# A four-layer block with attention and experts: maxima split by VectorE, squares by ScalarE, matrix steps at other hooks, rows of three tiles fetched at the border, first v products in group 0

## What is computed

```
x = x + attention(x)      # 16 heads of 16, masked softmax, projection Wo, RMS norm, gain and shift
x = x + experts(x)        # gate over 8 experts, best 2 of them, three layers 256-512-512-256 each, ReLU
x = x + spectral(x)       # x @ basis * cond -> orthogonalised 64x64 matrix -> * cond -> output basis
x = x + quaternions(x)    # fixed rotation of groups of features, gated
```

## Time and profile before

| | |
|---|---|
| median of three runs | 1247.67 us |
| profiled execution, its own time | 1257.77 us |
| its span | 1255.7 us |
| TensorE busy (PE) | 1152.4 us, 92% |
| VectorE busy (DVE) | 839.8 us, 67% |
| ScalarE busy (ACT) | 718.7 us, 57% |
| GpSimd busy (POOL) | 553.5 us, 44% |
| mean granted clock of TensorE | 0.977 |

### The profile page before, as it was taken

The page is one execution under the profiler, slowest core; times in us unless marked ns, Lnnn a source line. Parts: engine busy times, 40 slices in busy tenths (PEclk is TensorE's granted clock), DMA queues, the critical chain, the costliest instruction groups (busy, mean ns, idle before and its releaser), DMA issues.

```text
span 1255.7 us, 23441 instructions
## 1 busy us (share of the span) xinstructions
PE 1152.4 (92%) x7533; PEld 777.1 (62%) x7590; DVE 839.8 (67%) x2395; ACT 718.7 (57%) x1504; POOL 553.5 (44%) x869
## 2 busy tenths in 40 slices
PE   8899999989999899997877999878999999999978
PEld 4333434334344343432316989878999999999968
DVE  4888688897888978886843434535555567844447
ACT  3466666665656656564554556535555566566645
POOL 7324245674756748567372465441122212122210
PEclk9899999999999999998989999979999999999999
DMA  7835646348464484543535488942554666832636
GB/s 204 240 122 173 201 143 196 134 161 243 161 184 140 152 239 157 169 155 127 210 128 194 112 295 272 278 118 43 178 143 113 190 212 169 277 61 48 172 85 201
DMA packets 101456, 213.52 MB, mean 170 GB/s; under 512 B 10885, under 2 KB 71181, under 8 KB 92886
## 3 DMA queue, kind: packets, MB, share of 16 engines
q1 hardware_dynamic: 87030, 193.34, 47.5%
q0 software_dynamic: 14304, 18.69, 8.2%
HBM read 239.15 MB, written 74.29 MB: 250 GB/s over the span
## 4 chain that ended last, share of the span: by engine, by line
PE 65%; issue 7%; POOL 7%; DVE 7%; DMA 4%; SPq 4%; ACT 3%; another core or an unknown queue 1%; DVEq 0%; POOLq 0%; ACTq 0%
PE bank L1017 33%; PE bank L1117 6%; PE bank L1086 6%; PE bank L1098 5%; PE bank L1102 4%; PE bank L1062 3%; DVE junk L1534 2%; PE bank L1135 2%; SPq L876 2%; DMA w_parts<-in_W 2%; POOL ssq L790 1%; POOL xw L1803 1%; PE bank L1032 1%; ACT full L1336 1%; PE bank L1175 1%
## 5 line engine op out<-in xcount | busy, mean ns | idle before, releaser
L1272 ACT ACTIVATE pt<-bank 128x512 f32<-128x512 f32 x512 | 301.9, 596 | 191.9 <-PE bank L1102 137.9
L1534 DVE CUSTOM_DVE_ANT_0 junk<-bank,mneg 128x512 bf16<-128x512 f32 x512 | 336.4, 684 | 82.5 <-PE bank L1086 81.7
L1885 POOL DMA_INDIRECT x<-yout,rows x78 | 122.9, 1575 | 327.0 <-ACT yout L1341 309.8
L1681 DVE TENSOR_TENSOR hid<-full,hid 128x256 fp32r<-128x256 f32 x312 | 133.8, 432 | 170.1 <-ACT full L1336 158.4
L1017 PE MATMUL bank<-hid,w 128*128 128x256 f32 x1872 | 237.1, 284 | 6.9 <-DVE hid L1681 5.2
L1017 PEld LDWEIGHTS bank<-hid,w 128*128 128x128 f32 x1872 | 226.7, 191 | 7.7 <-issue 5.8
L1331 ACT ACTIVATE hid<-bank,biases 128x256 fp32r<-128x256 f32 x312 | 150.7, 483 | 127.5 <-PE bank L1017 106.3
L1336 ACT ACTIVATE full<-bank,biases 128x256 f32<-128x256 f32 x312 | 150.2, 481 | 0.0
L1102 PE MATMUL bank<-mneg,identb 128*128 128x512 bf16 x391 | 149.9, 383 | 0.0
L1017 PE MATMUL bank<-rowsT,w 128*128 128x256 f32 x936 | 128.9, 290 | 0.3 <-issue 0.3
L1117 PE MATMUL bank<-pt,vaug 128*17 128x512 f32 x1024 | 125.8, 610 | 2.2 <-ACT pt L1272 0.7
(11 more groups left out here) (184 smaller groups left out, 1479.4 us busy)
## 6 DMA issues: line engine op xcount, KB each, us to landing
w<-split_weights SPq DMA_DIRECT2D x80, 1024.0 KB
w<-split_weights SPq DMA_DIRECT2D x40, 2048.0 KB
split_weights<-w_parts SPq DMA_DIRECT2D x64, 512.0 KB, 4.8
w_parts<-in_W SPq DMA_DIRECT2D x64, 256.0 KB, 4.9
split_parts<-parts SPq DMA_DIRECT2D x28, 384.0 KB, 3.5
rows<-routed SPq DMA_DIRECT2D x39, 258.0 KB, 3.4
stacks<-split_parts SPq DMA_DIRECT2D x36, 256.0 KB, 7.5
qst<-split_parts SPq DMA_DIRECT2D x24, 256.0 KB, 7.5
```

Of the source, the lines that this page charges most:

```text
L1272: A.activation(pt[n % len(pt)][:, :], bank[3 + n % 2][:, :], ACT.Exp, scale=float(D) ** -0.5).then_inc(exped.sem, 1)
L1534: V.tensor_tensor_reduce(junk[n % 2][:, :], bank[n % 3][:, :], mneg[:, 0, st, :], 1.0, FLOOR, ALU.add, ALU.max, rowmax[gi % 2][:, hh, st:s ...
L1681: V.tensor_tensor(lo, h[:, :], hi.bitcast(F32), ALU.subtract).then_inc(hidden_low.sem, 1)
L1885: G.indirect_dma_start(x2_dram, bass.IndirectOffsetOnAxis(ap=rows[j % NS][:, tt, E + 1:E + 2].bitcast(U32), axis=0), yout[j % 2][:, tt], N ...
```

## The change

1. `split_maxima` is done by VectorE (one copy, then a subtraction that waits for it), at the same place in the list.
2. `square_o` and `square_x1` are done by ScalarE, as an activation Square with an accumulated output.
3. In `chain`, six empty hooks stand between `count` and `place` instead of four, and for batch 6 nine instead of six between `residual` and `scale`.
4. The v products of batch 0 leave the prologue and alternate in group 0 with the projections of batch 1; in the first two groups two entries of `todo` are worked off after each k.
5. The matrix steps stand after layer 2 steps 0 and 2, layer 1 step 1 and layer 3 step 0. Their generator yields four times before its first piece (`MATRIX_PAUSE`).
6. Fetching rows and fetching biases are steps of their own. At `near` the rows and biases of tile 0 and the rows of tile 1 are fetched; after the end of attention come rows and biases of tile 2, then biases and weights of tile 1, then tiles 3 and 4. The second rows buffer moves into the memory that is free at `near`, and both output buffers out of it.

```diff
--- before.py
+++ after.py
@@ -59,6 +59,7 @@
 CHUNKS = NX * W_ALL // CW
 CHUNK_BUFFERS = 3
 WARM = 12
+MATRIX_PAUSE = 4
 
 
 
@@ -121,7 +122,7 @@
         yield
         out.append(("square_o", b, st))
     out.append(("residual", b))
-    for _ in range(6):
+    for _ in range(9 if b == KNOWN else 6):
         yield
     for st in range(ST):
         out.append(("scale", b, st))
@@ -156,7 +157,7 @@
         if k == 0:
             yield
     out.append(("count", b))
-    for _ in range(4):
+    for _ in range(6):
         yield
     out.append(("place", b))
     yield
@@ -228,7 +229,7 @@
 
     def value_steps(b):
         steps = [("project_v", b, st) for st in range(ST)]
-        for n in reversed(range(STACK_STEPS)):
+        for n in reversed(range(STACK_STEPS if b else 0)):
             steps.insert(n + 1, ("stack", b, n))
         return steps
 
@@ -256,13 +257,11 @@
             out.append(("send", qk, half, part))
         if half == 0:
             out.append(("masks",))
-    for st in range(ST):
-        out.append(("project_v", 0, st))
     out.append(("constants",))
     for i in range(GROUPS + 3):
         b = i // NG
         if i % NG == 0 and b + 1 < B:
-            todo[:0] = project_steps(b + 1)
+            todo[:0] = project_steps(b + 1) if b else sum(zip(project_steps(1), value_steps(0)), ())
         if i == 0:
             todo += [("prepare",), ("modulation",)]
         if i % NG == (2 if b else 1) and b + 1 < B:
@@ -307,7 +306,7 @@
             if k == 3 and i == GROUPS - NG // 2:
                 out.append(("first_weights",))
             if (i, k) == (GROUPS, 1):
-                out.extend((("near",), ("fetch_rows", 0)))
+                out.extend((("near",), ("fetch_rows", 0), ("fetch_biases", 0), ("fetch_rows", 1)))
                 for layer in range(3):
                     out.append(("fetch_weights", layer, 0))
             if (i, k) == (GROUPS + 1, 2):
@@ -315,7 +314,7 @@
             if (i, k) == (GROUPS + 2, 0):
                 for m in range(HT):
                     out.append(("layer1", 0, m))
-            for _ in range(2 if len(todo) > 12 else 1):
+            for _ in range(2 if i < 2 or len(todo) > 12 else 1):
                 if todo:
                     work_off()
     out.extend(todo)
@@ -329,7 +328,7 @@
 
     def fetch_rows(j):
         if j < NTILES:
-            out.append(("fetch_rows", j))
+            out.extend((("fetch_rows", j), ("fetch_biases", j)))
 
     def add_output(j, tt):
         if j >= 0:
@@ -340,17 +339,18 @@
             next(side, out)
 
     out.append(("experts", "transfers"))
-    fetch_rows(1)
+    fetch_rows(2)
+    out.append(("fetch_biases", 1))
     for layer in range(3):
         fetch(layer, 1)
-    for j in range(2, NS):
+    for j in range(3, NS):
         fetch_rows(j)
     out.append(("quaternions",))
     fetch(0, 2)
     for j in range(NTILES):
         for m in range(HT):
             out.append(("layer2", j, m))
-            small_step(m % 2)
+            small_step(m % 2 == 0)
             if (j, m) == (0, 1):
                 out.extend((("experts", "engines"), ("turn", 1)))
         fetch(1, j + 2)
@@ -358,7 +358,7 @@
         for m in range(HT):
             if j + 1 < NTILES:
                 out.append(("layer1", j + 1, m))
-            small_step(m % 2 == 0)
+            small_step(m == 1)
         fetch(0, j + 3)
         for tt in range(TT):
             out.append(("layer3", j, tt))
@@ -423,6 +423,8 @@
     writer = Writer()
 
     def piece_by_piece():
+        for _ in range(MATRIX_PAUSE):
+            yield
         for _ in pieces:
             writer.extend(side)
             side.clear()
@@ -542,15 +544,16 @@
 
     def tile_buffers(i):
         return ([sb(f"rowsT{i}_{n}", [P, KT, TW], F32R) for n in range(2)], [sb(f"hid1_{i}_{n}", [P, HT, TW], F32R) for n in range(2)],
-                [sb(f"hid2_{i}_{n}", [P, HT, TW], F32R) for n in range(2)], sb(f"yout{i}", [P, TT, E]))
-
-    biases, rows = [sb("biases0", [P, B_ALL])], [sb("rows0", [P, TT, RW])]
+                [sb(f"hid2_{i}_{n}", [P, HT, TW], F32R) for n in range(2)])
+
+    biases, rows = [sb("biases0", [P, B_ALL])], [sb(f"rows{i}", [P, TT, RW]) for i in range(2)]
     full = [sb(f"full{i}", [P, TW]) for i in range(4)]
     first_tile_buffers = tile_buffers(0)
     w = [w0, sb("w1", [P, W_ALL // CW, 2, CW], F32R)]
-    rowsT, hid1, hid2, yout = zip(first_tile_buffers, tile_buffers(1))
+    rowsT, hid1, hid2 = zip(first_tile_buffers, tile_buffers(1))
+    yout = [sb(f"yout{i}", [P, TT, E]) for i in range(2)]
     biases += [sb(f"biases{i}", [P, B_ALL]) for i in range(1, NS)]
-    rows += [sb(f"rows{i}", [P, TT, RW]) for i in range(1, NS)]
+    rows += [sb(f"rows{i}", [P, TT, RW]) for i in range(2, NS)]
     quat = sb("quat", [P, KT, E])
     obm = sb("obm", [KB, E])
     basis = sb("basis", [P, E])
@@ -978,6 +981,9 @@
                     sp.wait_ge(dma_add, 16 * TT * (j - NS + 1))
                 row = nc.sync.value_load(table[0:1, j:j + 1], min_val=0, max_val=NULL_ROW)
                 start(rows[n][:, :, :], routed[bass.ds(row, TW), :].rearrange("(t p) c -> p t c", p=P)).then_inc(dma_rows[n], 16)
+            elif name == "fetch_biases":
+                j, = at
+                n = j % NS
                 expert = nc.sync.value_load(table[0:1, NTILES + j:NTILES + j + 1], min_val=0, max_val=NX - 1)
                 start(biases[n][:, :], d["biases"][bass.ds(expert, 1)].rearrange("e p c -> p (e c)")).then_inc(dma_biases[n], 16)
             elif name == "quaternions":
@@ -1224,6 +1230,12 @@
 
     def scalar_program(engine):
         act = Queue(engine)
+
+        def square(sums, src, n):
+            if n >= 2:
+                act.wait_ge(squares.sem, n - 1)
+            A.activation(squared[n % 2][:, :], src, ACT.Square, accum_out=sums).then_inc(squares.sem, 1)
+
         for step in order:
             name, *at = step
             if name == "project":
@@ -1280,6 +1292,16 @@
                 else:
                     act.wait_ge(masks_made, 4)
                 A.activation(osb[:, st, :], ps[:, 0:E], ACT.Copy).then_inc(o_ready.sem, 1)
+            elif name == "square_o":
+                b, st = at
+                act.wait_ge(*o_ready.at((b, st)))
+                if b:
+                    act.wait_ge(*rooted.at(("residual", b - 1)))
+                square(ssq[:, 0, st:st + 1], osb[:, st, :], squares.value[step] - 1)
+            elif name == "square_x1":
+                b, st = at
+                act.wait_ge(*rooted.at(("normalised", b)))
+                square(newton[:, 0, st:st + 1], xw[0][:, st, 0:E], squares.value[step] - 1)
             elif name == "turn_x1":
                 b, k = at
                 ps, _ = misc_bank(step)
@@ -1375,11 +1397,6 @@
         def gate_step(op, *args, **kw):
             op(*args, **kw).then_inc(gate_dve.sem, 1)
             gate_n[0] += 1
-
-        def square(sums, src, n):
-            if n >= 2:
-                dve.wait_ge(squares.sem, n - 1)
-            V.tensor_tensor_reduce(squared[n % 2][:, :], src, src, 1.0, 0.0, ALU.mult, ALU.add, sums).then_inc(squares.sem, 1)
 
         def side_stage(step):
             name, *at = step
@@ -1533,6 +1550,17 @@
                     dve.wait_ge(*max_split.at((gi - 2,)))
                 V.tensor_tensor_reduce(junk[n % 2][:, :], bank[n % 3][:, :], mneg[:, 0, st, :], 1.0, FLOOR, ALU.add, ALU.max,
                                        rowmax[gi % 2][:, hh, st:st + 1]).then_inc(max_found.sem, 1)
+            elif name == "split_maxima":
+                gi, = at
+                found = rowmax[gi % 2][:, :, :]
+                first_part, second_part = (m2[gi % 2][:, :, k * GH:(k + 1) * GH].rearrange("p s h -> p h s") for k in range(SHIFTS))
+                dve.wait_ge(constants_made, CONSTANTS)
+                dve.wait_ge(*max_found.at((gi, GH - 1, ST - 1)))
+                if gi >= 2:
+                    dve.wait_ge(*max_turned.at((gi - 2,)))
+                V.tensor_copy(first_part, found).then_inc(max_split.sem, 1)
+                dve.wait_ge(*max_split.at((gi,), 1))
+                V.tensor_tensor(second_part, found, first_part, ALU.subtract).then_inc(max_split.sem, 1)
             elif name == "clear":
                 gi, kt, hh = at
                 pr = pt[col_place[gi, kt, hh] % len(pt)]
@@ -1565,22 +1593,12 @@
                 if b >= 2:
                     dve.wait_ge(*o_projected.at((b - 2, ST - 1)))
                 V.transpose(oT[b % 2][:, gi % NG // 2, :], turned[0][:, :, :].rearrange("p a c -> p (a c)")).then_inc(normal.sem, 1)
...
             elif name == "gate_max":
                 b, = at
                 dve.wait_ge(*gate_pool.at(("logits", b)))
@@ -1737,17 +1755,6 @@
                 pool.wait_ge(*middle.at((b, qk, half)))
                 G.tensor_tensor(parts[qk][:, half, 2, :], rest[n % 2][:, :], parts[qk][:, half, 1, :],
                                 ALU.subtract).then_inc(lows.sem, 1)
...
             elif name == "constants":
```

21 lines of the change are left out of this document (removed).

## The result

The changed kernel takes 1217.5 us (median of 4 runs, 1216.4 to 1219.4), the one before beside it 1247.3 (1245.4 to 1255.2): ratio 0.975, 95% interval 0.971 to 0.979, or 29.8 us less. The profiled execution of the changed kernel took 1216.96 us (span 1215.2). That of before took 1257.77, so the two profiles differ by 40.8 us, 11 more than the medians.

A forecast was written before the change was run, and what follows sets the result against it. TensorE was taken to set the pace, so only its waits count. The terms summed to -30.3 us, 1227.5 from the profiled 1257.8; 28 us carried to the median gave 1220 us, range 1204 to 1241.

The forecast's parts named there:

- hooks and pause: Tile loop: large products between eliminations end TensorE's waits, -15.3 us; the pause avoids part of the longest wait, -2 us.
- v products (to group 4): Start: an earlier first row gains nothing, new waits for bank and modulation come; +2 us, ends -4 and +5.
- split and squares: Attention: split on VectorE ends a 6.6 us stall, -5 us; squares on ScalarE relieve VectorE, -5 us.
- border: Turn from attention to tiles: the wait for rows 2 goes, that for rows 1 is handed on; -2 us.
- place: Last placing in the expert part: two more hooks cover TensorE's 3.52 us wait for GpSimd's counts; -3 us.
- in the last tile: Tile loop: matrix steps were to end by tile 38 of 39; running into the last tile would show an error.
- The ScalarE rival: Attention: ScalarE becomes the bound in the trains of exponentials, 56 squares by 0.5 us = 28 us; 1261 us, chance 0.07.
- ScalarE idled less before them: Attention: the forecast is wrong if ScalarE idles less at its exponentials and TensorE waits for them; no size given.
- the whole 13.8 us: Attention: TensorE's 20.4 us of waits less the 6.6 us stall, the most that moving the squares could win.
- the 41 us of the rival: Squares in attention: Square needs its own table, two loads for each of 16 runs; 1261 us and more, chance 0.02.
- the queue of transfers: End of attention: SyncE's chunk stores stand behind its wait for batch 5's scatters; 1.6 us of the split's gain given back.
- the rival in which only the matrix waits go: Whole kernel: VectorE's relief fills no stall and single stalls return elsewhere; 1247.7 - 15 = 1233 us, chance 0.22.

The follow-up runs named there:

- the kernel with the hooks alone: The kernel before with only the matrix steps at the new hooks and the pause of four; 1225.5 us on chip B.
- A's kernels with the new hooks: The changed kernel on chip A with squares back on VectorE (1253.3 us), split back on GpSimd (1238.5) or v products back ahead of group 0 (1236.6).
- before's attention: Attention as in the kernel before, traced in that kernel with only the new matrix-step hooks and the pause of four; 1225.5 us on chip B.
- both undone: The changed kernel with squares back on VectorE and the split of the maxima back on GpSimd; 1248.1 us on chip C.

## Why the prediction was right, and where its steps were not

The forecast was 1220 us, 28 under before, and 1217.5 came. The mechanism that I gave more than half of the sum did it. The parts beside it were off in both directions and cancelled, and that they did is luck. On chip B, from the marks of the kernel with the hooks alone to those of the changed kernel:

```
step                                 forecast      measured (chip B unless said)
hooks and pause                      -15.3 - 2     -22.7
v products (to group 4)              +2            +6.4   (84.9 against 78.5)
split and squares (group 4 - tile 0) -5 - 5        -5.3   (573.1 against 578.4)
border                               -2             0     (waits 5.4 against 5.7)
tiles 0 to 10, place                 -3            -5.8   (140.2 against 146.0)
tile 10 to the end, other than hooks  0            -0.6
sum                                  -30.3         -28.0  (medians: -28.3)
```

The border lies within tiles 0 to 10, so its zero is not added. The 5.8 us of that stretch are not the place hooks' either: with them undone on B it takes 140.5 us, and with the border undone 141.3. Which part wins them no run shows.

**Hooks.** Right in mechanism and place: two large products between steps cover the 2.25 us, the tile with four eliminations takes 12.7 us (895.8 to 908.5 between two turns) in place of 14.3, and the last matrix step's product starts at 1158.1 us, in the last tile; I had named that as a sign of error. From the last turn to the end it takes 74.9 us now and 72.0 before, but TensorE's waits for the last stage's matrices (rcob) are 3.6 us in both. The size was low. Behind tile 13 the kernel before waits only 12.8 us at eliminations, in 11 waits, and the loop still gave 17.6, since tiles behind the last elimination got shorter as well: those at 1071.7 and 1096.9 took 13.4 and 15.9 us, and now none there takes over 11.8. And what lies ahead of tile 13, where I gave the pause 2 us, came to 5.1 on B by difference; no run has the pause alone. Undone in the changed kernel, the first eliminations run into ScalarE's stop and both together cost 10.1 us of waiting. I had reasoned that TensorE would soon have stopped there for ScalarE anyhow. On C that is so, and in A's kernels with the new hooks: they wait there as well. On B the stop does not come at all.

**Squares.** This step failed as I put it on the chip of the result. I priced VectorE's relief at 5 us of TensorE's waits for row maxima; between 60 and 560 us they are 13.7 us with before's attention and 14.6 in the changed kernel, and in the first two profiles 20.4 and 20.4. Two things in it were off. The relief was 7.5 us of VectorE in 500 us on B (418.0 to 410.5) and not 20 in 530, in part because the split costs VectorE 0.66 us a time, 21.2 in all, and not 0.4 and 12.8. And the longest wait is still the scale step that stands for GpSimd's root (the earlier trace rows showed 6.72 us); why the other 13 to 15 us did not shrink on B is not shown. That step reads now:

```profile
579.25 0.79 DVE L1600 SCALAR_TENSOR_TENSOR osb<-osb,ssq,gain_shift 128x256 f32<-128x256 f32 x1 [5.28 <-POOL ssq L793]
```

On C the waits fell from 14.5 to 6.3 us with squares and split together, and time by 8.7. The ScalarE rival did not come: TensorE's waits for exponentials rose by only 2.6 us, though ScalarE idled less before them (178.2 us in the changed kernel's first profile, 191.9 in the earlier trace rows), which I had named as a sign of error. A square holds ScalarE for 0.39 us and not for the 0.6 of its records, but 56 of them would still be 22 us; that so little of it reaches TensorE fits the gaps between trains that I had set against the rival, and no run tests it. The prediction cited the Trainium skill, SBUF — State Buffer, section Who interferes with whom, by which the move would take the whole 13.8 us. The squares of osb did run longer on VectorE than those of x1 (701 against 436 ns with both undone on C) and run alike on ScalarE (412 and 423), which agrees with the rule. The profile of before shows it square by square: 14 squares of osb with no GpSimd instruction beside them took 413 ns on average, and the two longest, 2.36 and 2.59 us, ran beside GpSimd's tensor_tensor of xin. The time that the rule would give did not come.

**Activation table.** One load of 1283 ns stands in the profile after, as before, so neither the 41 us of the rival nor the estimate of 85 came.

**Split.** The wait of 4.7 us at the turn is gone as forecast. I had named the queue of transfers as what is late next. On A it was GpSimd all the same: undoing the split there brought the wait back and took another of 4.4 us away. I had given 1.6 us back for this; by that run it is all of it, within some 5 us. On B the traces read otherwise: from group 4 to tile 0 the waits for row maxima are 24.6 us with before's attention and 24.2 in the changed kernel, the 4.1 us for the split maxima are gone, and the stretch is 5.3 us shorter at a mean clock of 0.985 in place of 0.979. So there the whole gain of the row is the split's stall with the half clock behind it, as forecast, and the squares' share is nothing.

**V products.** The sign was right, the size a third of what came up to group 4. I had written that an earlier first row gains nothing because ScalarE's copy waits for the 24 sends, and then counted only the new waits of the bank and the modulation as 2.4 us; they were 1.9 to 2.4 and 3.3. What I did not ask is what the 5.36 us of v products had been covering: the first row product waits 4.9 us for the stacks now. A product moved out of a wait leaves the wait.

**Border and place.** Both waits moved as written, the sum over the run did not. At the border the weights of tile 1 are issued 0.9 us later than with the border undone (675.01 against 674.16), near the 1.1 that I had counted. But TensorE then waits once for 5.4 us in place of twice for 5.7 together, with a granted clock of 0.50 (the 1.2 GHz level) for the 5 us behind it, and reaches the turn of rows 2 at 688.2 us against 688.5: the wait for rows 2 was not won, it was moved ahead. The place hooks removed their 3.4 us and cost as much elsewhere.

**The sum against one execution.** I carried 28 of 30.3 us to the median because some of the counted stalls might be that execution's own. The runs say it better: from tile 10 on that profile is spaced like the one of chip C (52.9 and 400.4 us against 52.8 and 400.4), and on C the change brings 18.2 us, about what I gave the rival in which only the matrix waits go (15). A forecast of 1220 for a chip of the other kind was right by two errors, in the start and in attention, that took back what the hooks gave more.

## What to carry to other kernels

Where one engine is at its pace, the safe gain is a dependent pair of small steps taken apart until the products between them outlast the latency of one: behind tile 13 it came to the same 382.7 to 382.8 us on three chips and with and without the other parts, where the kernel before takes 400.4. Single stalls between queues are handed on more often than removed: border, place and, on chip A, split each moved their wait and none moved the total. Before work is moved out of a prologue, ask which transfer it was covering.

## What the runs showed that I had not expected

The chips differ. One program took 1219.9 us on B and 1239.4 on C, and the one before 1248.2 and 1257.6, so the worth of a change depends on the chip, 28.3 us here and 18.2 there. On C and A engines stop for nothing that the profile names. ScalarE stops beside GpSimd's scatters at the end of placing, 7.8 us at once on C, in the kernel before as well, and twice, by 4.2 and 6.4 us with the split undone, on A. TensorE stops 8.9 us in 7 waits from 60 to 560 us in the changed kernel on C, at 258, 336 to 338, 418 to 420 and 501 to 503 us, so every 79 to 83 us; on B and in the kernel before on C it does not. By size that would be most of the 10 us by which the change is worth less on C. What these stops are, and which part of the change brings TensorE's, stays open. The Trainium skill, Runtime: NRT & Kernel Launch, section Instruction fetch mechanics, says that each engine refills its instructions by a DMA queue of its own, mostly hidden; no run here shows that the stops are such refills, and nothing was run to tell.

ScalarE's accumulating activation shows as two records, 412 and 197 ns for 128x256, and occupies the queue for 0.39 us.
